# The V product of an attention kernel in two column halves of TensorE's array, four key blocks at a time

## What is computed

```python
q = (hidden_states @ Wq.T).reshape(B, Sq, H, HD).transpose(0, 2, 1, 3)
...
qr = apply_rope(q, cos, sin)
kr = apply_rope(k, cos, sin)
draft = jnp.einsum('bhqd,bhkd->bhqk', qr, kr)
...
_, draft_indices = jax.lax.top_k(draft, num_remain)
...
scores = jnp.einsum('bhqd,bhkd->bhqk', qr, kr) / np.sqrt(HD).astype(np.float32) + mask
attn = jax.nn.softmax(scores, axis=-1)
out = jnp.einsum('bhqk,bhkd->bhqd', attn, v)
```

## Time and profile before

| | |
|---|---|
| median of 3 runs | 4231.47 us (4231.04 to 4231.67) |
| span of the profiled execution, first to last instruction | 4232.6 us |
| TensorE matmuls busy | 3367.7 us, 80% |
| VectorE busy | 3153.8 us, 75% |
| ScalarE busy | 2685.2 us, 63% |
| GpSimd busy | 2008.4 us, 47% |
| phase A, B, C | 610, 3243, 380 us |

### The profile page before, as it was taken

The page is one execution under the profiler, slowest core; times in us unless marked ns, Lnnn a source line. Parts: engine busy times, 40 slices in busy tenths (PEclk is TensorE's granted clock), DMA queues, the critical chain, the costliest instruction groups (busy, mean ns, idle before and its releaser), DMA issues. The chain is left out here.

```text
span 4232.6 us, 55872 instructions
## 1 busy us (share of the span) xinstructions
PE 3367.7 (80%) x15864; PEld 1556.6 (37%) x15864; DVE 3153.8 (75%) x6185; ACT 2685.2 (63%) x4577; POOL 2008.4 (47%) x5916
## 2 busy tenths in 40 slices
PE   6999947787688677886877688888677888887998
PEld 3444423333233333332333233333333333333444
DVE  4667758888788688987876888888688888772333
ACT  1222137788588688886876688888688888872111
POOL 1222236555357665544576555546675554572000
PEclk9999968898899788998987899999878899998998
DMA  3112120000010110001001000010010000002211
GB/s 113 64 63 80 60 57 17 11 9 9 7 21 16 24 26 12 10 7 21 13 18 32 12 10 10 9 21 13 23 29 12 10 7 9 12 15 94 75 75 45
DMA packets 221756, 124.01 MB, mean 29 GB/s; under 512 B 188164, under 2 KB 206852, under 8 KB 221316
## 3 DMA queue, kind: packets, MB, share of 16 engines
q1 hardware_dynamic: 221316, 119.36, 10.0%
HBM read 76.28 MB, written 42.99 MB: 28 GB/s over the span
## 5 line engine op out<-in xcount | busy, mean ns | idle before, releaser
L901 PE MATMUL banks<-pT,v_sb 128*65 128x512 f32 x2176 | 1182.2, 627 | 30.9 <-ACT oT L1005 29.6
L990 ACT ACTIVATE pT<-banks 128x512 f32<-128x512 f32 x1088 | 634.2, 591 | 514.4 <-PE banks L873 509.2
L848 PE MATMUL banks<-k_sb,q_sb 128*128 128x512 bf16 (+3 forms) x1280 | 504.6, 394 | 380.1 <-DVE sc L1156 344.1
L1156 DVE TENSOR_SCALAR_CACHE_REDUCE sc<-banks 128x1024 f32<-128x1024 f32 (+7 forms) x768 | 674.9, 904 | 70.6 <-PE banks L853 39.2
L1183 DVE MAX8 near<-keys 128x8 f32<-128x256 f32 (+14 forms) x480 | 653.5, 1361 | 17.2 <-DVE keys L1181 0.6
L981 ACT ACTIVATE junk<-sc,tt 128x256 fp8e4<-128x256 f32 (+14 forms) x480 | 597.5, 1246 | 54.0 <-POOL tt L1048 53.9
L981 ACT ACTIVATE junk<-sc,t_all 128x256 fp8e4<-128x256 f32 (+14 forms) x480 | 599.3, 1249 | 33.9 <-DVE sc L1156 32.0
L981 ACT ACTIVATE junk<-sc,tiny 128x256 fp8e4<-128x256 f32 (+14 forms) x480 | 595.3, 1246 | 11.8 <-DVE sc L1168 11.8
L867 PE MATMUL banks<-q_sb,k_sb 128*128 128x512 bf16 x1088 | 444.1, 408 | 189.8 <-ACT pT L990 69.2
L850 PE MATMUL banks<-k_sb,q_sb 96*128 96x512 bf16 (+3 forms) x1280 | 494.1, 396 | 0.0
L873 PEld LDWEIGHTS banks<-eye,mk 128*128 128x128 bf16 x4352 | 358.6, 103 | 299.3 <-issue 68.9
(11 more groups left out here) (247 smaller groups left out, 4885.9 us busy)
## 6 DMA issues: line engine op xcount, KB each, us to landing
q_sb<-scratch_qk SPq DMA_DIRECT2D x896, 32.0 KB, 1.9
scratch_qk<-parts SPq DMA_DIRECT2D x16, 960.0 KB, 3.7
a_x<-in_x SPq DMA_DIRECT2D x16, 512.0 KB, 4.2
scratch_x<-a_x SPq DMA_DIRECT2D x16, 512.0 KB, 2.9
scratch_attn<-o_sb SPq DMA_DIRECT2D x128, 64.0 KB, 1.6
c_xn<-scratch_attn SPq DMA_DIRECT2D x16, 512.0 KB, 3.7
c_x<-scratch_x SPq DMA_DIRECT2D x16, 512.0 KB, 4.6
out<-c_x SPq DMA_DIRECT2D x16, 512.0 KB, 2.6
```

The lines of the kernel that those rows point to most:

```text
L848: nc.tensor.matmul(r_slot(n)[:, j:j + wj], q_sb[:, p % QS, 0, h, :], k_sb[:, group[p] % 2, 0, col:col + wj], start=True, stop=False)
L901: nc.tensor.matmul(psum[0:VP, 6, :], v_sb[:, group[p] % 2, kb, :], pT[:, n % PTS, :], start=(kb == 0), stop=(kb == blocks[p] - 1)).then_in ...
L990: nc.scalar.activation(pT[:, tn % PTS, :], psum[:, 4 + n % 2, :], ACT.Exp, scale=SCALE)\
L1156: v.tensor_scalar(sc[:, p % SCS, h, c * CHUNK:c * CHUNK + w], r_slot(n)[:, 0:w], 0.0, None, ALU.add, ALU.max, accum_out=mx[:, p % 4, c, h: ...
```

## The change

- The V product of a key block becomes two products, each of two heads (256 columns) with V's 33 columns. One writes partitions 0 to 32 of bank 6, the other partitions 64 to 96: they use the left and the right half of the array's columns.
- They are issued for up to four key blocks together (`BATCH`), once all four are at least three blocks old, or, with `rest`, for what is left of a place. The blocks keep their order; `pT` has eight buffers instead of four.
- `oT` is now 128 partitions by 256 columns instead of 65 by 512: the copy has half the columns, and two 128x128 transposes take the place of four of 65x65. VectorE reads their result in another order.
- V in SBUF has 33 columns instead of 65.

```diff
-VP = 65
+HALF = P // 2
+PAIRS = REP // 2
...
-QS, SCS, PTS = 5, 3, 4
+QS, SCS, PTS = 5, 3, 8
+BATCH = 4
...
-FLAGS = REP * VP
+FLAGS = PAIRS * P
...
-        oT = sb("oT", [VP, REP * P])
+        oT = sb("oT", [P, PAIRS * P])
...
-                def values(upto):
+                def values(upto, rest):
                     while done_pv[0] <= upto:
                         n = done_pv[0]
-                        done_pv[0] += 1
                         p = max(q for q in range(N) if blocks_before[q] <= n)
+                        many = min(BATCH, blocks_before[p + 1] - n)
+                        if n + many - 1 > upto and not rest:
+                            break
+                        many = min(many, upto - n + 1)
+                        done_pv[0] += many
                         kb = n - blocks_before[p]
-                        pe.wait_ge(sm["ex"], unit_no["T", p, kb] + 1)
+                        pe.wait_ge(sm["ex"], unit_no["T", p, kb + many - 1] + 1)
...
-                        nc.tensor.matmul(psum[0:VP, 6, :], v_sb[:, group[p] % 2, kb, :], pT[:, n % PTS, :],
-                                         start=(kb == 0), stop=(kb == blocks[p] - 1)).then_inc(sm["pv"], 1)
+                        for k in range(many):
+                            for half in range(2):
+                                last = nc.tensor.matmul(
+                                    psum[half * HALF:half * HALF + VW, 6, 0:PAIRS * P], v_sb[:, group[p] % 2, kb + k, :],
+                                    pT[:, (n + k) % PTS, half * PAIRS * P:(half + 1) * PAIRS * P],
+                                    start=(kb + k == 0), stop=(kb + k == blocks[p] - 1))
+                            last.then_inc(sm["pv"], 1)
...
-                    for h in range(REP):
-                        last = nc.tensor.transpose(psum[:, 7, h * VP:(h + 1) * VP], oT[:, h * P:(h + 1) * P],
-                                                   b.eye[0:VP, 0:VP])
+                    for m in range(PAIRS):
+                        last = nc.tensor.transpose(psum[:, 7, m * P:(m + 1) * P], oT[:, m * P:(m + 1) * P], b.eye[:, :])
...
-                        values(blocks_before[p] + kb - LAG)
+                        values(blocks_before[p] + kb - LAG, False)
                         if seen == min(LAG, blocks[p]):
-                            values(blocks_before[p] - 1)
+                            values(blocks_before[p] - 1, True)
...
-                    nc.scalar.activation(oT[:, :], psum[0:VP, 6, :], ACT.Copy).then_inc(sm["ot"], 1)
+                    nc.scalar.activation(oT[:, :], psum[:, 6, 0:PAIRS * P], ACT.Copy).then_inc(sm["ot"], 1)
...
-                    acc = psum[:, 7, 0:REP * VP].rearrange("p (h d) -> p h d", h=REP)
-                    link(v.reciprocal(rec[:, :], acc[:, :, HD]))
+                    acc = psum[:, 7, 0:PAIRS * P].rearrange("p (m s d) -> p m s d", m=PAIRS, s=2)
+                    link(v.reciprocal(rec[:, :, :], acc[:, :, :, HD]))
```

More of the change, by code:

```diff
@@ L722, in phase_b @@
         k_sb = sb("k_sb", [P, 2, 2, S], BF16)
-        v_sb = sb("v_sb", [P, 2, TILES, VP])
+        v_sb = sb("v_sb", [P, 2, TILES, VW])
         sc = sb("sc", [P, SCS, REP, S])
@@ L748, in phase_b @@
         heads_bad = sb("heads_bad", [P, REP])
-        rec = sb("rec", [P, REP])
+        rec = sb("rec", [P, PAIRS, 2])
         o_sb = sb("o_sb", [P, 2, REP, HD])
@@ L960, in _ @@
                     if j == N:
-                        values(blocks_before[N] - 1)
+                        values(blocks_before[N] - 1, True)
                     if j == N + 1:
@@ L1142, in _ @@
                 link(v.tensor_scalar(wide_steps[:, 8:16], b.steps[:, 0:8], 8.0, None, ALU.add))
-                link(v.memset(v_sb[:, :, :, HD:VP], 1.0))
+                link(v.memset(v_sb[:, :, :, HD:VW], 1.0))
                 v.memset(k_sb[ONES_AT:ONES_AT + PARTS_OF_MAX, :, 1, :], 1.0).then_inc(sm["fill"], 1)
@@ L1302, in normalise @@
                     dve.wait_ge(sm["otr"], p + 1)
-                    acc = psum[:, 7, 0:REP * VP].rearrange("p (h d) -> p h d", h=REP)
-                    link(v.reciprocal(rec[:, :], acc[:, :, HD]))
+                    acc = psum[:, 7, 0:PAIRS * P].rearrange("p (m s d) -> p m s d", m=PAIRS, s=2)
+                    link(v.reciprocal(rec[:, :, :], acc[:, :, :, HD]))
                     if p >= 2:
                         dve.wait_ge(written[p % 2], 16 * (p // 2))
-                    v.tensor_tensor(o_sb[:, p % 2, :, :], acc[:, :, 0:HD],
-                                    rec[:, :].rearrange("p (h o) -> p h o", o=1).broadcast_to([P, REP, HD]),
+                    v.tensor_tensor(o_sb[:, p % 2, :, :].rearrange("p (s m) d -> p m s d", s=2), acc[:, :, :, 0:HD],
+                                    rec[:, :, :].rearrange("p m (s o) -> p m s o", o=1).broadcast_to([P, PAIRS, 2, HD]),
                                     ALU.mult).then_inc(sm["norm"], 1)
```

## The result

The changed kernel takes 4121.5 us (4117.5 to 4126.3, four runs) against 4231.3 us before: a ratio of 0.974, 95% interval 0.9726 to 0.9754. It is faster, by 110 us. The forecast was 4008, 223 us less than before, with a range from 3895 to 4170. So sign and range hold, but the gain is just under half of what was forecast, and the forecast's reason for it was too generous. The time is that of the rival "handed back by the clock and the bursts" (4122); whether for its reasons is for the experiments.

A forecast was written before the change was run, and what follows sets the result against it. Phase B was taken as bound by a ring of waits, closed in wide steps by ScalarE's work plus its waits for TensorE. TensorE saves 335 us (936 - 537 - 64), 224 reach the end: 4008 us, range 3895 to 4170.

The forecast's parts named there:

- handed back by the clock and the bursts: Rival: TensorE idles more, one more half-clock passage costs 1.3 us in 88 wide steps, +114, 4122 us; chance 0.18.
- Ring and bound: Phase B: three engines about 80% busy wait in a ring, closed in wide steps by ScalarE's work plus waits for TensorE.
- Two halves: V product on TensorE: matmuls on different column halves overlap, 0.43 us a block instead of 0.86; 537 us instead of 936.
- The unpaired slot: V product: one 0.215 us matmul slot per batch has no partner, 320 batches, 69 us.
- average step of 12 blocks: TensorE's saving of 335 us, 0.31 a block, expressed as 3.7 us in an average step.
- Changes of form: TensorE's array goes into and out of halves each batch: 640 changes at 0.10 us, 64 us (58 to 160).
- Batches: Up to four blocks' V products together: hold TensorE's queue 2.1 us against 0.86; up to 1.2 us where cover is missing.
- ScalarE's cover of 2.6 us: Work in the two banks while a batch holds TensorE's queue: an exponential of 0.6 and a count of 1.99 us.
- the first rival: Halves run one after the other: V stays 0.86 us a block, plus changes of form, +80, 4312 us; chance 0.11.
- Copy to `oT`: End of a place: smaller copy saves 26 us, ScalarE's longer wait for up to four products costs 24; they cancel.
- What reaches the end: Phase B waits of VectorE that go: `directions` 150, score banks 28, transposes 26, `second_update` 20; 224 us in sum.
- The wide step that I worked out: Step at 3380.4 us, 38.4 long: ScalarE's round becomes 35.0, 3.4 of VectorE's 4.31 us gap go; the 1.65 wait stays.

The follow-up runs named there:

- half_v_alone: Kernel before with its V product cut to the first two heads (256 of 512 columns), no batches or changes of form: 4088.0 us, ratio 0.965.
- the filler: Changed kernel plus 28 idle 128-column matmuls before the third head's scores (a step's second ones) in places of over 1024 columns: 4170.2 us, ratio 0.985.

## Why the prediction was right and wrong

- **Ring and bound.** Right that none of the three engines is the bound and that ScalarE's round, its work and its waits for TensorE, closes the ring in wide steps. ScalarE's wait for transposed scores (509 to 428 us) and that of `directions` (200 to 137) shrink together, as this reading says, but far less than the 300 and 50 that were forecast; VectorE's share of phase B is 84%, not 88.
- **Two halves.** Right: pairs 7 ns apart, 0.43 us a block as forecast. The unpaired slot, 69 us, was wrong. The "average step of 12 blocks" was a slip too: a place has 8.5 blocks on average (1088 in 128), 2.6 us of the 335; nothing else was worked out from it.
- **Changes of form.** 0.10 each, read from L141, was right: 0.23 us a batch for two. At full clock that makes 1088 x 0.43 + 320 x 0.23 = 542 us instead of 936: 394 us less, more than the 335 forecast. As the phases ran, with their half-clock stretches, it was 1025 - 561 = 464, less the 30 on the units ahead.
- **Batches.** They had no term of their own, since ScalarE's cover of 2.6 us exceeds what a batch holds. In the change they cost some 20 us (two against four), and not for want of that cover: nearly all of it lies before the copy to `oT`. At full width they cost 128. I had put that price at 35 us in the first rival (1 us in 0.4 of the wide steps): had the halves not overlapped, that rival's 4312 would have been too low by some 90 (128 - 35), by this run.
- **Copy to `oT`.** It takes 0.38 us instead of 0.58, 0.2 as forecast. ScalarE's wait before it grew by 3 us, not 24; but with half the product and no batches it fell from 84 to 49 us, and with two at a time to 57. So the burst at a place's end did cost some 30, and the faster product hid it.
- **What reaches the end: the step that failed.** I wrote that "most of the others shrink, since TensorE now reaches each block's scores 0.3 us earlier" and took three quarters of the 200 us of `directions`. It came to 63 (200 to 137). The other terms: score banks 6 of 28 (55.6 to 50.0), transposes 14 of 26 (52.3 to 38.6), `second_update` 8 of 20 (102.5 to 94.1). Together 91 of 224, and the span fell by 108. The fault is the same in all: I scaled the waits by how much earlier TensorE would be, and did not ask what TensorE does during them. It was at the V product in 151 of ScalarE's 651 us and in 49 of VectorE's waits. That these 200 are a ceiling is what the runs show: 110, 145 and 177 us came back with 464, 443 and 854 us off the product. In proportion they give 91 for the change, near the 110 measured, but also only 86 for `half_v_alone`, which gained 145; so how the waits come back within the ceiling is open. The rest of the waits is units, scores and stands for VectorE, which a faster V product does not shorten and the last of which it lengthens (stands before score banks 344 to 386 us).
- **The wide step that I worked out** was to lose 3.4 us and lost 0.6. I let the wait of 1.65 us stay; it became 3.76, because after TensorE's longer stand the scores behind it ran at half clock (with the filler in that stand it was 1.84). That is a reading for this step and one more like it; the 64 steps of tiles 8 to 15 lost 1.5 us on average.
- **The rival with the same time, 4122.** The clock fell, 0.89 to 0.84, though not to the 0.8 or less that was its sign, and the time at half clock rose from 733 to 1018 us. TensorE was busy in 642 of them, 504 before; at full clock the difference would take 69 us less, and of ScalarE's waits 24 us more pass at half clock, 12 of them due to it. The rival's 114 us are one more half-clock passage in each of 88 steps. The scores at the start of a step run at half clock in 14 more of the 64 steps of tiles 8 to 15, those of the second head in 2 more. So most of its reason was not what happened; the number was met by chance. How much the clock costs in sum is not settled: one filler removed a passage that only few steps have, the other took off 49 us at half clock of 1018, and no experiment raised the clock over the whole phase.

## What to carry to other kernels

Before a faster operation is priced, take the waits of the engines behind it and add up which instructions the waited-for engine executes during them; only those in which it executes the operation that is to be made faster are up for saving. Here they were a fifth of it (200 of 1025 us), and none of the three runs with a cheaper product gave back more. A run with the operation nearly removed tells how much there is to gain (177 us) for the price of one kernel. Look for the cost of a batch where an engine waits for its last piece: here before the copy at the end of a place. And work that is moved into a stand leaves a new one where it came from.

## What the runs showed of the hardware

- f32 matmuls of 33 output columns, one on partitions 0 to 32 and one on 64 to 96, start 7 ns apart, and such a pair starts every 216 ns for 256 columns. The Trainium skill, "TensorE: Matmul & The Clock Gate", The mechanism, says in one sentence that weight loads overlap running matmuls only where the row group differs; the same section also lets a load for the background weight buffer go ahead of them. Here the loads (111 ns in the median) run under matmuls on the same rows, 16 of them in a batch of 1.85 us, so the first sentence does not hold in this trace.
- Going into column halves and out costs 0.23 us: 0.09 to 0.10 on the last matmul before, 0.03 in the first slot, 0.10 in the last. The Trainium skill, "TensorEngine Tiling (Array Packing)", Key Properties, says that a change of tiling mode drains TensorE, without a figure; that the 0.23 us are this drain is likely and not shown.
- Two microseconds of standing (1.99, before the second scores) were followed by eight matmuls at 1.2 GHz (0.43 us for 512 columns); with matmuls in the same stand they ran at 2.4 GHz (0.22 us).
